# Storing 15 of 40 widened mask pieces in DRAM and loading them back, in a four-layer graph network kernel

## The reference

```python
# layer 0: per-node weights, Chebyshev terms I, A, 2AA - I
x = layernorm(x + gnn0(x, adj, embedding, weight, bias))
# layer 1, twice: h = adj @ z ; z = relu(h @ w_i)
x = layernorm(x + gnn1(x, adj))
# layer 2: x @ w_self + (adj @ x) @ w_neighbor + bias
x = layernorm(x + gnn2(x, adj))
# layer 3: [x, Ax, 2AAx - x, Ax, 2AAx - x] @ weight + bias
x = layernorm(x + gnn3(x, adj, adj))
```

## Time and profile before

| quantity | value |
|---|---|
| median of three runs | 1265.39 us |
| the profiled execution | 1266.25 us, span 1264.4 us |
| PE matmul busy | 1177.2 us, 93% |
| DVE busy | 939.7 us, 74% |
| ACT busy | 475.1 us, 38% |
| POOL busy | 403.5 us, 32% |
| mean DMA rate | 84 GB/s |

### The profile page before, as it was taken

One profiled execution on the slowest core, in us unless ns is written; L12 is line 12 of the kernel. 1 busy time (PEld: TensorE's weight loads), 2 busy tenths in 40 slices (PEclk: granted clock), 3 DMA queues, 4 the chain that ended last, 5 costly groups with the idle time before them and its releaser, 6 DMA issues.

```text
span 1264.4 us, 16665 instructions
## 1 busy us (share of the span) xinstructions
PE 1177.2 (93%) x5539; PEld 970.0 (77%) x5539; DVE 939.7 (74%) x1932; ACT 475.1 (38%) x646; POOL 403.5 (32%) x250
## 2 busy tenths in 40 slices
PE   9999999999999998998999988989898899989793
PEld 6888888888888886776878867767677688878682
DVE  5845888786688778995156487979898885747788
ACT  6631111011112111111276647465554655554562
POOL 0001111111116444560235241425445373633320
PEclk9999999999999999998999998989999999999896
DMA  9731121321133212213400101002222266672221
GB/s 366 300 101 59 44 69 46 94 73 55 38 84 117 63 59 63 63 63 98 167 1 7 61 20 48 1 9 64 63 51 51 51 163 154 148 186 76 67 67 61
DMA packets 168206, 106.53 MB, mean 84 GB/s; under 512 B 120048, under 2 KB 140048, under 8 KB 166832
## 3 DMA queue, kind: packets, MB, share of 16 engines
q1 hardware_dynamic: 168112, 105.38, 28.5%
HBM read 68.64 MB, written 36.70 MB: 83 GB/s over the span
## 4 chain that ended last, share of the span: by engine, by line
PE 58%; DVE 22%; issue 8%; SPq 5%; ACT 3%; DMA 3%; DVEq 0%; POOL 0%; ACTq 0%
PE ps L1572 19%; PE ps L1172 8%; PE ps L1459 8%; PE ps L1460 8%; PE ps L1174 8%; SPq L1394 4%; PE ps L1477 3%; DVE nat L1862 2%; DVE B L1221 2%; DVE sml L1316 2%; DVE ring L1862 2%; DVE ops L1278 2%; PE ps L1507 2%; ACT ops L1248 2%; PE ps L1508 2%
## 5 line engine op out<-in xcount | busy, mean ns | idle before, releaser
L1172 PE MATMUL ps<-B,ops 128*128 128x512 f32 x1008 | 405.1, 402 | 32.0 <-ACT B L1217 19.5
L1174 PE MATMUL ps<-B,ops 128*128 128x512 f32 x1008 | 396.6, 393 | 0.0
L1572 PE MATMUL ps<-Tw,xs 128*128 128x512 f32 x1280 | 309.5, 391 | 8.0 <-DVE ring L1862 7.9
L1572 PEld LDWEIGHTS ps<-Tw,xs 128*128 128x128 f32 x1280 | 238.1, 188 | 65.0 <-DVE ring L1862 9.7
L1217 ACT CAST B<-pk 128x1024 fp32r<-128x1024 fp8e4 x225 | 228.5, 1044 | 99.6 <-PE ps L1174 99.5
L1172 PEld LDWEIGHTS ps<-B,ops 128*128 128x128 f32 x1008 | 192.1, 191 | 77.3 <-ACT B L1217 21.6
L1174 PEld LDWEIGHTS ps<-B,ops 128*128 128x128 f32 x1008 | 192.1, 191 | 37.6
L1219 POOL CAST B<-pk 128x1024 fp32r<-128x1024 fp8e4 x90 | 115.4, 1282 | 285.1 <-PE ps L1174 264.0
L1459 PE MATMUL ps<-B,xs 128*128 128x512 f32 x512 | 200.9, 392 | 0.0
L1460 PE MATMUL ps<-B,xs 128*128 128x512 f32 x512 | 199.9, 390 | 0.0
L1862 DVE SCALAR_TENSOR_TENSOR nat<-ps,embn,nat 128x128 f32<-128x128 f32 x448 | 153.9, 344 | 40.5 <-PE ps L1572 39.7
(11 more groups left out here) (117 smaller groups left out, 1321.5 us busy)
## 6 DMA issues: line engine op xcount, KB each, us to landing
raw<-in_at SPq DMA_DIRECT2D x10, 1024.0 KB, 15.5
td<-raw SPq DMA_DIRECT2D x31, 256.0 KB, 2.7
raw<-in_at SPq DMA_DIRECT2D x12, 512.0 KB, 8.6
zd<-nat SPq DMA_DIRECT2D x24, 256.0 KB, 2.9
stg<-zd SPq DMA_DIRECT2D x24, 256.0 KB, 5.1
tb<-stq SPq DMA_DIRECT2D x40, 128.0 KB, 2.1
pk<-tb SPq DMA_DIRECT2D x5, 1024.0 KB, 7.6
td<-ring_g SPq DMA_DIRECT2D x17, 256.0 KB, 2.0
```

What stands on the lines that cost most here:

```text
L1172: pe.matmul(bank, ops[:, slot, 0, m, :], of, start=not more and m == 0, stop=False, skip_group_check=more)
L1174: mm = pe.matmul(bank, ops[:, slot, 1, m, :], of, start=False, stop=m == 7, skip_group_check=more)
L1572: mm = pe.matmul(ps[:, 4 + 2 * p + q, :], src, Tw[:, wi, 512 * p:512 * p + 512], start=i == 0, stop=i == 4)
```

## The change

Five edits:

1. `EXPANDS` becomes a table by step. In the first group pass (step 2) ACT widens 25 pieces and DVE 15. In the passes of steps 3, 4 and 6 ACT widens 25, and the other 15 (`D`) are not widened at all. In step 5 ACT widens 35 and DVE 5. POOL widens none.
2. `stash`: in the first group pass SP stores the 15 pieces that DVE has widened to a DRAM tensor `tf`, 512 KB each; the next user of that place of the ring waits until the store has landed.
3. A `D` piece is loaded from `tf` by a DMA that ACT issues, in the order of its other steps, when product e-5 has ended.
4. The square, the root and the `unit` get steps of their own. Except in the last pass the square stands one slot later than before and at the slot's end (rank 9), `deviation` one slot later, the root two slots later, and `unit` at `weigh` + 5. The last pass has `LAST_WEIGH` in place of `WEIGH` and no added slots.
5. In `handover` the rest of group 2's products, and the steps behind them, move behind four quarters of group 3's.

```diff
+EXPANDS = {2: "AAVAAVAV", 3: "AADAADAD", 4: "AADAADAD", 5: "AAAAAAAV", 6: "AADAADAD"}
+STASHED = [k for k in range(40) if EXPANDS[6][k % 8] == "D"]
...
+LAST_WEIGH = [17, 18, 21, 22, 25, 26, 29, 30]
...
+    for x, w in enumerate(LAST_WEIGH if n == len(PASSES) - 1 else WEIGH):
...
         put(t, 2, "expand", *u)
+        if e in STASHED:
+            put(t + 2, 1, "stash", *u)
...
+        late = n < len(PASSES) - 1
...
                 put(w + 1, 4, "mean", j, p, c)
-                if behind:
-                    put(w + 1, 5, "unit", *behind)
...
-                put(w + 2, 5, "deviation", j, p, c)
-                behind = j, p, c
...
+                put(w + 1 + late, 9, "square", j, p, c)
+                put(w + 2 + late, 4, "deviation", j, p, c)
+                put(w + 2 + 2 * late, 5, "root", j, p, c)
+                put(w + 3 + 2 * late, 5, "unit", j, p, c)
...
+                def wait_piece(eng, e):
+
+                    if e < len(RING):
+                        eng.wait_ge(s_prod, n_first)
+                        return
+                    eng.wait_ge(s_unit, unit_at[Step("product", *SPREAD[e - len(RING)])])
+                    if e - len(RING) in stash_at:
+                        eng.wait_ge(*stash_at[e - len(RING)])
...
+                    if s.kind == "expand" and expand_at[Unit(s.j, s.p, s.c, s.k)][1] == "D":
+                        u = Unit(s.j, s.p, s.c, s.k)
+                        e, _, signal, _ = expand_at[u]
+                        wait_piece(ac, e)
+                        ac.wait_ge(*stash_at[e % 40])
+                        ac.dma_start(B[:, piece_of(u), 0:1024].bitcast(F32), tf[STASHED.index(e % 40)]).then_inc(signal, 16)
...
+                    if s.kind == "stash":
+                        u = Unit(s.j, s.p, s.c, s.k)
+                        e = expand_at[u][0]
+                        sp.wait_ge(*expand_at[u][2:])
+                        sp.dma_start(tf[STASHED.index(e)], B[:, piece_of(u), 0:1024].bitcast(F32)).then_inc(stash_at[e][0], 16)
...
         closing(3, 3)
-        for _ in products:
-            pass
...
                 put("mm", 3, 2, c, m)
                 if t == -15:
                     put("split", 3, 2, 3)
+                if t == -13:
+                    for _ in products:
+                        pass
```

More of the change, by code:

```diff
@@ L445 @@
 KEPT = {0: 2, 1: 1, 2: 0}
-EXPANDS = "AAPAAPAV"
+EXPANDS = {2: "AAVAAVAV", 3: "AADAADAD", 4: "AADAADAD", 5: "AAAAAAAV", 6: "AADAADAD"}
+STASHED = [k for k in range(40) if EXPANDS[6][k % 8] == "D"]
 RING = [8, 9, 10, 11, 15]
@@ L469, with expander @@
 WEIGH = [18, 21, 24, 27, 30, 33, 36, 39]
+LAST_WEIGH = [17, 18, 21, 22, 25, 26, 29, 30]
+def expander(e):
+    return EXPANDS[PASSES[e // 40][1]][e % 8]
 def chunks(n):
     g, p = PASSES[n]
-    for x, w in enumerate(WEIGH):
+    for x, w in enumerate(LAST_WEIGH if n == len(PASSES) - 1 else WEIGH):
         _, b, half = SUMS[x // 2]
@@ L553, in second_part @@
                     put(t0 + at, 8, "refill", 2 * g + b, p, 2 * half + q)
-        behind = None
+        late = n < len(PASSES) - 1
         for j, _, c, w in chunks(n):
@@ L570, in second_part @@
                 put(w + 1, 4, "mean", j, p, c)
-                if behind:
-                    put(w + 1, 5, "unit", *behind)
-                    if p == 6:
-                        put(w + 2, 9, "ship", *behind)
-                put(w + 2, 5, "deviation", j, p, c)
-                behind = j, p, c
-        if behind:
-            put(w + 3, 5, "unit", *behind)
+                put(w + 1 + late, 9, "square", j, p, c)
+                put(w + 2 + late, 4, "deviation", j, p, c)
+                put(w + 2 + 2 * late, 5, "root", j, p, c)
+                put(w + 3 + 2 * late, 5, "unit", j, p, c)
             if p == 6:
-                put(w + 4, 9, "ship", *behind)
+                put(w + 4 + 2 * late, 9, "ship", j, p, c)
     return {t: [s for _, s in sorted(of, key=lambda e: e[0])] for t, of in events.items()}
@@ L598, with gnn_stack @@
 Way = namedtuple("Way", "pe act dve pool sp act_start dve_start sp_start sp_end")
-def gnn_stack(nc, xn, x0, xt, at, rb, r16, emb, embt, b0, w01, w2, wbd, bias, eye, eps, out, zd, y1d, bd, td, tb):
+def gnn_stack(nc, xn, x0, xt, at, rb, r16, emb, embt, b0, w01, w2, wbd, bias, eye, eps, out, zd, y1d, bd, td, tb, tf):
     from contextlib import ExitStack
@@ L993, in second_way @@
                 lane_at = {s.c: i + 1 for i, s in enumerate(complete) if (s.j, s.p) == (2, 2)}
-                expand_at, n_of = {}, {"A": 0, "P": 0, "V": 0}
+                s_ring = s_r + [s_at[4][1], s_at[0][1], s_p]
+                n_ring = [had_st + 16 * 20] * 2 + [16, 32, max(part_at.values())]
+                expand_at, stash_at, n_of = {}, {}, {"A": 0, "P": 0, "V": 0}
                 for e, u in enumerate(SPREAD):
-                    by = EXPANDS[e % 8]
-                    n_of[by] += 1
-                    expand_at[u] = e, by, n_of[by]
+                    by, i = expander(e), e % len(RING)
+                    if by == "D":
+                        n_ring[i] += 16
+                        expand_at[u] = e, by, s_ring[i], n_ring[i]
+                    else:
+                        n_of[by] += 1
+                        expand_at[u] = e, by, {"A": s_exA, "P": s_exP, "V": s_exV}[by], n_of[by]
+                    if e in STASHED:
+                        n_ring[i] += 16
+                        stash_at[e] = s_ring[i], n_ring[i]
                 stored_at, turned_at, n_slot = {}, {}, [had_tw] * N_TURN
@@ L1149, in pe_step @@
                         if i in PACKED:
-                            _, by, v = expand_at[u]
-                            pe.wait_ge({"A": s_exA, "P": s_exP, "V": s_exV}[by], v)
+                            pe.wait_ge(*expand_at[u][2:])
                         slot = operand_slot(n, i)
@@ L1199, in pe_step @@
                         mm.then_inc(s_four, 1)
+                def wait_piece(eng, e):
[5 more added lines that the diff above has]
+                        eng.wait_ge(*stash_at[e - len(RING)])
                 def expanded(eng, s, by):
                     u = Unit(s.j, s.p, s.c, s.k)
-                    e = expand_at[u][0]
                     b = PACKED[s.p]
                     eng.wait_ge(s_pk, had_pk + (64 if b < 4 else 80))
[L1207 to L1210, removed]
+                    wait_piece(eng, expand_at[u][0])
                     if b < 4:
@@ L1257, in act_step @@
                         ac.activation(home(j, c), ps[:, wbank_of[s._replace(kind="weigh")], :], ACT.Relu).then_inc(s_evict, 1)
-                    if s.kind == "mean":
-                        ac.wait_ge(s_mean, mean2_at[s])
+                    if s.kind == "square":
+                        ac.wait_ge(s_mean, mean2_at[s._replace(kind="mean")])
                         ac.activation(ps[:, wbank_of[s._replace(kind="weigh")], :], home(j, c), ACT.Square).then_inc(s_sq, 1)
-                    if s.kind == "deviation":
+                    if s.kind == "root":
                         sm = stats(j, c)
-                        ac.wait_ge(s_var, dev_at[s])
+                        ac.wait_ge(s_var, dev_at[s._replace(kind="deviation")])
                         ac.wait_ge(s_const, 32)
@@ L2166 @@
     args.append(nc.dram_tensor("tb", (5, P, 8 * 1024), F8).ap())
+    args.append(nc.dram_tensor("tf", (len(STASHED), P, 1024), F32).ap())
     gnn_stack(nc, *args)
```

## The result

Beside each other on one chip the kernel before took 1266.05 us and the changed one 1253.97 us (medians of four each, 1264.2 to 1267.46 and 1251.88 to 1255.29). The ratio is 0.9904 with an interval of 0.9884 to 0.9924. It is faster by 12 us. The forecast was 1236.4 us: the sign was right and the time lies in the range, but less than half of the 29 us came.

The account below looks back on a forecast made before the run. PE was taken as the bound, with gains where it idles or runs slowly. Terms -6 - 20 - 9 - 6 - 3 + 12 + 3 = -29 us from 1266.25 gave a median of 1236.4 us, range 1216 to 1264.

Parts of the forecast that it names:

- Handover: At 588 us, four quarters of group 3's product fill PE's wait for an eviction: -6 us, bounds -7.5 and 0.
- Squares later: In the passes, later squares and lighter DVE work cut 25 us of PE waits and slow clock: -20, bounds -25 and 0.
- The tail: After the last product, weighing earlier lets DVE work without gaps: -3 us, bounds -8 and 0.
- DVE's widenings make PE wait: In the second part PE waits 12.4 us for DVE's widenings; most in normalising passes go: -9 us, bounds -12 and -5.
- the relief of POOL: POOL loses 90 widenings, 115.4 us, which matters only because DVE is stretched when both work on SBUF.
- turned chunks, -6: Of PE's 17.6 us waiting for turned chunks from DRAM, faster DVE saves 6 us; bounds -12 and +6.
- loads, +12: In six passes, 78 tight loads take 4.5 us against windows of 4.2: +12 us, from nothing to +98.
- the table's net 0: The new table's terms: DVE widenings -9, turned chunks -6, loads +12, the rest (stores, first pass, step 5) +3.
- Loads land too late: Rival: loads contend with refills and turned chunks and hold PE, deciding above a 5.25 us mean landing; 1286 us, chance 0.15.
- ACT stays the bottleneck: Rival: waits only change place, ACT staying as busy, so the later squares' 20 us are not won; 1256 us, chance 0.17.
- Loads are free: Rival: loads land in under 4.2 us and cost nothing; 1224 us, down to 1215 with more clock regained, chance 0.18.
- No wait of 5 us in a pass's second block product: Sign of being right: PE's waits of 5 us or more there, 18.1 us over three passes, would be gone.

Follow-up runs that it names:

- e6_poolinstead: The change with POOL widening the 15 pieces of a normalising pass that were loaded, so no loads: 1227.04 us, 0.9700 of the kernel before.
- e2_noload: The change with the old table of widenings, nothing stored or loaded, all moved steps kept: 1235.52 us, 0.9751 of the kernel before.
- e7_actmore: The change without loads, old table, but ACT takes DVE's pieces in normalising passes (30 ACT, 10 POOL): 1216.54 us, 0.9621 of the kernel before.
- e5_quarter: The change with each load moving 128 KB instead of 512 KB, part of the computation left out: 1227.95 us, 0.9718 of the kernel before.
- e10_spissue: The change with SP issuing the 90 loads instead of ACT, at the same slots: 1255.11 us, 0.9905 of the kernel before.
- e4_oldsq: The change with squares, roots and units at their old slots in all passes but the last: 1274.92 us, 1.0063 of the kernel before.

## Why the prediction was right in sign and wrong in size

**Right: the moved steps.** *Handover*: -6 forecast, 6.7 measured, and the place looks as drawn. *Squares later*: -20 forecast, 16.5 to 19.4 measured. *The tail*: -3 forecast, 5.9 to 8.3 measured, at the far bound of 8; the tail of 26.0 us was forecast near 23 and is 18.2. These three were -29 in the sum and are 31.5 us together. The tail was mis-sized by a factor of two or more, on the good side.

**Right: that DVE's widenings make PE wait**, 12.4 us before and 1.3 after, and that taking them off DVE pays. But e6_poolinstead shows it without any load: the new table with POOL gains 6.5 us over e2_noload. Its waits show 18.4 us for DVE turn into 2.0 for DVE and 9.6 for ACT. Nearly all of the 9.6 stands in the three holes and right behind them, not in step 5, where ACT widens 35 pieces and fits, as costed.

**Not needed: the relief of POOL.** That POOL's widenings stretch DVE's work was the reason to expect something from loads. DVE's busy time is 20.6 us longer in e6_poolinstead than in the change (927.3 against 906.7), so the stretching is there. But the fastest kernel, e7_actmore, keeps POOL's 90 widenings, and e5_quarter, with POOL as free as the change, is no faster than e6_poolinstead. What the relief alone would bring stays open: no run takes these widenings off POOL without loads in their place, and e5_quarter's own waits for loads can hide a gain.

**Wrong: the terms "turned chunks, -6" and "loads, +12"**, and with them the whole of the table's net 0, which measured +19.3. Without the loads the sum was -41, and e6_poolinstead measures -38.0; the loads were +12 and cost 25.8. The failed step is in how the loads were priced: at what PE waits for the loads themselves. The sum took nothing for what they do to the others.

Even the part that was priced came near by luck. Issue lateness and landing were put at 4.5 us and are 4.43 in the trace (0.28 + 4.15), and the 12 us of waits are 17.1. But the 12 were to be 78 windows, each a little short. In the trace 14 waits are long enough to be listed, and two of them, 9.2 of the 17.1 us, stand behind loads that ACT issued 4.1 and 4.3 us late, where the lateness was put at 0.5 us for all.

What was missing is what 47 MB of loads do to everything else that moves:

1. The turned chunks wait 25.6 us instead of 15.9 in e6_poolinstead and 17.6 before. My term had -6, with +6 only as a bound; against before it is +8.
2. PE's clock. Waits of 5 us and more are back at 755.60 and 899.81, each with a stretch at the 1.2 GHz level behind it (a clock of 0.50 and 0.58 over the next 5 us); PE's busy time is 11.0 us above that of e6_poolinstead. Part of the slow clock that the moved steps had removed came back with the loads: PE's busy time is 1177.2 us before, 1172.7 in e2_noload and 1180.3 in the change.

In the profiled executions these add up. Loads, turned chunks and widenings of ACT and DVE, and DVE's eviction (line 1318), make 46.2 us of PE's waits in the change and 32.8 in e6_poolinstead, a difference of 13.4; with 11.0 of busy time it is 24.4 of the 25.7 us between the spans. This split is read from the two traces; no run separates the waits from the clock. That the bytes cause both is shown by e5_quarter, whose turned chunks wait 11.3 us and whose PE is busy 1170.5.

**The rivals.** "Loads land too late" had the right mechanism, contention with refills and turned chunks, and the wrong condition. It was to decide at a mean of 5.25 us to landing; the mean is 4.43 and the cost of the loads was 25.8 us, more than twice the forecast's. The Trainium skill, "DMA: Bandwidth & Descriptors" (Issuing engines are not separate DMA queues), says that transfers of different issuers run on the same 16 engines and interleave; e10_spissue agrees, with 12.0 us of gain against 12.2 from another issuer. "ACT stays the bottleneck" (1256) is nearest to the measured time by chance: the later squares bring 20.2 us beside the loads too (e4_oldsq), so its 20 us were not what was lost. One piece of it is there, in the two holes behind ACT's late issues. "Loads are free" fell: they cost 25.8 us.

**What was to show it.** Of the forecast's signs, the missing wait at 588, POOL without widenings, and DVE's vanished waits came true. "No wait of 5 us in a pass's second block product" failed at 755.60, and that line alone said that the loads had taken the place of what they were to cure. The clock in the step-3 pass, 0.95, stands at the limit that I had set. The landings near 4 us came true as a median, but 15 of the 90 took over 5.

## What to carry to other kernels

In this kernel DMAs put in place of work on an engine cost less by their own landing time than by what their bytes did to the small, urgent transfers around them: before trading widenings for loads, list every other transfer in the same stretch with its slack, and shrink the bytes once as an experiment. An engine's busy time is no reason to relieve it, unless something waits for it: the fastest kernel here still widens 90 pieces on POOL. Moving the instruction at which an in-order engine gets stuck, here the square, gave as much (16.5 and 20.2 us with the two tables tried) as moving widenings from DVE to ACT (16.5, e7_actmore against e2_noload).

## What the runs showed of the hardware

- A store of 512 KB from SBUF to DRAM lands in 2.6 us (median of 15), a load of the same piece in 4.0 (3.1 to 7.1, median of 90), and a load of 128 KB in 2.3. The stores came in a pass in which hardly any other transfers run (19 GB/s without them, in e6_poolinstead), so direction and neighbours are not told apart.
- While the DMA engines moved 260 GB/s at a share of 0.74, a load of 512 KB took 6.3 us. The mean share over the step-6 pass is 0.80 at 222 GB/s; its turned chunks (64 KB) are those that came late, up to 7.4 us against 4.9 before and 5.0 in e5_quarter.
- Which engine issues a load decides who waits (17.1 us for loads and 25.6 for turned chunks from ACT's queue, 33.9 and 5.3 from SP's), not how much is lost (1253.97 and 1255.11 us).
